# Splitting the weights one expert ahead and taking the first batch in two halves, in an attention and expert-MLP kernel

## What is computed

```
a  = layernorm(x);  xn = layernorm(a) * gamma + beta
q, k, v = split(xn @ w_qkv);  k = softmax over the tokens(k)      # 4 heads of 32
att = (k^T v per head) applied to q, @ w_out + b_out
x1 = x + layernorm(att + a)
h  = layernorm(x1)
x2 = x1 + layernorm(sum over 8 experts of (silu(h @ Wg[e]) * (h @ Wu[e])) @ Wd[e])
```

## Time and profile before

| | |
|---|---|
| median of 3 runs | 592.81 us (592.29 to 592.82) |
| the profiled execution | 592.07 us |
| its span in the trace | 590.3 us |
| TensorE busy (matmuls) | 583.4 us, 99% of the span |
| VectorE, ScalarE, GpSimd busy | 74%, 59%, 29% |

### The profile page before, as it was taken

The page is one execution under the profiler, slowest core; times in us unless marked ns, Lnnn a source line. Parts: engine busy times, 40 slices in busy tenths (PEclk is TensorE's granted clock), DMA queues, the critical chain, the costliest instruction groups (busy, mean ns, idle before and its releaser), DMA issues.

```text
span 590.3 us, 9190 instructions
## 1 busy us (share of the span) xinstructions
PE 583.4 (99%) x2627; PEld 462.7 (78%) x2627; DVE 437.8 (74%) x975; ACT 346.0 (59%) x619; POOL 170.8 (29%) x205
## 2 busy tenths in 40 slices
PE   9999999999999999999999999999999999999996
PEld 5677887788877888778878788778887788888885
DVE  5877885798667985779756887678875787668666
ACT  5778666545574555745557556654567545555554
POOL 4997680037001370015500353004610032001001
PEclk9999999999999999999999999999999999999999
DMA  5522110201101020100202002020110201010000
GB/s 164 159 75 89 37 36 1 73 19 54 37 36 37 19 70 22 59 31 1 89 0 72 18 19 71 1 72 19 37 37 0 73 18 37 1 37 18 2 0 19
DMA packets 28032, 24.46 MB, mean 41 GB/s; under 512 B 3024, under 2 KB 20944, under 8 KB 27984
## 3 DMA queue, kind: packets, MB, share of 16 engines
q1 hardware_dynamic: 27408, 23.73, 12.5%
q10 hardware_dynamic: 576, 0.20, 0.1%
HBM read 15.27 MB, written 8.65 MB: 41 GB/s over the span
## 4 chain that ended last, share of the span: by engine, by line
PE 96%; ACT 1%; DVE 1%; issue 1%; POOL 0%; POOLq 0%; DVEq 0%; ACTq 0%
PE gate_ps L985 10%; PE gate_ps L988 10%; PE up_ps L988 10%; PE acc_ps L988 10%; PE gate_ps L986 10%; PE up_ps L985 10%; PE acc_ps L985 10%; PE up_ps L986 10%; PE acc_ps L986 10%; PE att_ps L1066 1%; PE att_ps L1077 1%; PE att_ps L1052 1%; PE up_ps L1125 1%; PE att_ps L1043 0%; PE att_ps L1073 0%
## 5 line engine op out<-in xcount | busy, mean ns | idle before, releaser
L587 ACT ACTIVATE gs<-gate_ps 128x512 f32<-128x512 f32 x255 | 152.4, 598 | 217.0 <-PE gate_ps L988 215.8
L795 DVE TENSOR_TENSOR h<-gs,up_ps 128x512 f32<-128x512 f32 x255 | 174.8, 685 | 131.3 <-PE up_ps L988 119.2
L782 DVE TENSOR_TENSOR h_lo<-h,h_hi 128x512 fp32r<-128x512 f32 x255 | 187.8, 736 | 0.1
L564 ACT ACTIVATE h_hi<-h 128x512 fp32r<-128x512 f32 x255 | 159.4, 625 | 8.9 <-DVE h L795 8.9
L985 PE MATMUL gate_ps<-x1nT_hi,wg_hi 128*128 128x512 f32 (+1 forms) x256 | 106.6, 416 | 0.0
L988 PE MATMUL up_ps<-x1nT_lo,wu_hi 128*128 128x512 f32 (+1 forms) x256 | 101.4, 396 | 0.0
L988 PE MATMUL gate_ps<-x1nT_lo,wg_hi 128*128 128x512 f32 (+1 forms) x256 | 101.4, 396 | 0.0
L985 PE MATMUL up_ps<-x1nT_hi,wu_hi 128*128 128x512 f32 (+1 forms) x256 | 101.0, 395 | 0.0
L988 PE MATMUL acc_ps<-h_lo,wd_hi 128*128 128x512 f32 x254 | 100.8, 397 | 0.0
L986 PE MATMUL gate_ps<-x1nT_hi,wg_lo 128*128 128x512 f32 (+1 forms) x256 | 100.6, 393 | 0.0
L986 PE MATMUL up_ps<-x1nT_hi,wu_lo 128*128 128x512 f32 (+1 forms) x256 | 100.5, 393 | 0.0
(11 more groups left out here) (228 smaller groups left out, 492.3 us busy)
## 6 DMA issues: line engine op xcount, KB each, us to landing
w_raw<-in_L_ffn_Wg_dram SPq DMA_DIRECT2D x8, 256.0 KB, 2.8
w_raw<-in_L_ffn_Wu_dram SPq DMA_DIRECT2D x8, 256.0 KB, 2.8
w_raw<-in_L_ffn_Wd_dram SPq DMA_DIRECT2D x8, 256.0 KB, 3.2
x_in<-in_L_attn_x_dram SPq DMA_DIRECT2D x7, 256.0 KB, 2.6
t_dram_acc<-t_blk_acc SPq DMA_DIRECT2D x7, 256.0 KB, 2.3
t_out_acc<-t_dram_acc SPq DMA_DIRECT2D x28, 64.0 KB, 2.0
out_dram<-res SPq DMA_DIRECT2D x7, 256.0 KB, 2.1
t_dram_x<-t_blk_x SPq DMA_DIRECT2D x6, 256.0 KB, 2.1
```

Of the source, the lines that this page charges most:

```text
L564: act.activation(h_hi[s % NH][:, :], h[s % NGU][:, :], ACT.Copy).then_inc(s_hhi, 1)
L587: act.activation(gs[q][:, :], gate_ps[q][:, :], ACT.Silu).then_inc(s_silu, 1)
L782: dve.tensor_tensor(h_lo[s % NH][:, :], h[s % NGU][:, :], h_hi[s % NH][:, :].bitcast(F32), ALU.subtract).then_inc(s_hlo, 1)
L795: dve.tensor_tensor(h[q][:, :], gs[q][:, :], up_ps[q][:, :], ALU.mult).then_inc(s_h, 1)
```

## The change

It has these parts. `FIRST` becomes 1: only expert 0 is split in the prologue, and each later expert 4 steps later than before (expert e from step 4(e-1) on), on ScalarE and GpSimd; the tables of the attention stay. GpSimd's low part 1 moves ahead of the powers of z and x1. The steps 0 and 1 of the MLP (`EARLY = 2`) run in halves, the first half's high products ahead of the second half's transposes. In the prologue the first two tiles go ahead of the last two through the statistics, variance and mean of x, z and x1; x1 is made in SBUF and its copy falls away; one of each pair of x1n tiles is made by ScalarE in two instructions; the last y tile moves from ScalarE to VectorE; a residual matmul moves behind the matmuls of A; and 20 fillers on zeros become 10 matmuls on weight data in five forms and 3 on zeros. The load of batch 2's x waits for the x1 sums and no longer for their copies.

```diff
@@ -38,10 +38,12 @@
-BUSY = {"start": 8, "w": 5, "attn": 20}
-FIRST = 2
+BUSY = {"start": 8, "w": 5}
+FIRST = 1
+EARLY = 2
@@ -359,7 +362,7 @@
                 if m == 8:
-                    sp.wait_ge(s_f_x1, J)
+                    sp.wait_ge(s_f_x1ps, J)
                     load_x(2, 0)
@@ -495,17 +498,18 @@
                 toks = slice(i * JH, i * JH + JH)
-                pool.wait_ge(s_f_y, i * JH + JH)
+                pool.wait_ge(s_f_y, JH + i)
+                if i == 1:
+                    pool.wait_ge(s_f_y_dve, 1)
                 pool.tensor_tensor(yb[:, toks, :], y[:, toks, :], bout_bc[:, :].rearrange("p (a d) -> p a d", a=1)
...
             split_lo(pool, 0)
+            split_lo(pool, 1)
             half_power("z", 0)
             half_power("z", 1)
-            split_lo(pool, 1)
             half_power("x1", 0)
             half_power("x1", 1)
-            for m in range(2, 3 * FIRST):
-                split_lo(pool, m)
+            split_lo(pool, 2)
             bodies(pool, body)
@@ -630,10 +634,9 @@
             act.activation(Ek[:, JH:, :], gate_ps[0][:, HALF], ACT.Copy).then_inc(s_f_E2, 1)
-            residual(3)
+            split_hi(0)
             act.wait_ge(s_f_qT_ps, 1)
             act.activation(qT[:, :], acc_ps[:, :], ACT.Copy).then_inc(s_f_qT, 1)
-            split_hi(0)
             split_hi(1)
@@ -641,12 +644,24 @@
                                    bias=nm["z"][:, j:j + 1], scale=1.0).then_inc(s_f_zc, 1)
-            for m in range(3, 3 * FIRST):
-                split_hi(m)
             act.wait_ge(s_mask, 3)
...
+            def first_x1n(i):
+                j = i * JH + 1
+                act.wait_ge(s_f_nm, 3 + i)
+                act.activation(x1n[:, j, :], x1[0][:, j, :], ACT.Identity, bias=nm["x1"][:, j:j + 1],
+                               scale=1.0).then_inc(s_f_zc, 1)
+                act.wait_ge(s_f_zc, J + 1 + i)
+                act.wait_ge(s_f_rstd["x1"], i + 1)
+                act.activation(x1n[:, j, :], x1n[:, j, :], ACT.Copy,
+                               scale=rstd["x1"][:, 0, j:j + 1]).then_inc(s_f_x1n_act, 1)
+            first_x1n(0)
             act.wait_ge(s_f_n, 1)
             act.activation(x1nT_hi[0][:, HALF], att_ps[:, HALF], ACT.Copy).then_inc(s_f_hi, 1)
+            first_x1n(1)
             act.wait_ge(s_f_n, 2)
@@ -846,11 +861,11 @@
             first_stats("x", 1, x_in[0][:, 1, :])
+            first_aggregate("x", 0)
+            first_variance("x", 0, 1)
             dve.wait_ge(s_xb, 16)
             first_stats("x", 2, x_in[0][:, 2, :])
-            first_aggregate("x", 0)
             first_stats("x", 3, x_in[0][:, 3, :])
-            first_variance("x", 0, 1)
             first_aggregate("x", 1)
@@ -872,6 +887,9 @@
             dve.tensor_reduce(kmax_neg[:, 0:1], att_ps[:, :], AX_X, ALU.max, negate=True).then_inc(s_f_kmax, 1)
+            dve.wait_ge(s_f_nmr, 1)
+            dve.tensor_scalar(y[:, J - 1, :], x_in[0][:, J - 1, :], rstd["x"][:, 0, J - 1:J], nmr[:, J - 1:J], ALU.mult,
+                              ALU.add).then_inc(s_f_y_dve, 1)
             dve.wait_ge(s_f_T, 1)
@@ -889,64 +907,57 @@
-            def z_mean(i):
+            def half_mean(k, i):
                 toks = slice(i * JH, i * JH + JH)
-                dve.tensor_scalar(nm["z"][:, toks], mv["z"][:, toks, 0], -1.0, None, ALU.mult).then_inc(s_f_nm, 1)
-            for j in range(3):
-                dve.wait_ge(s_f_z, j + 1)
-                first_stats("z", j, tile_banks[j][:, 0:D])
-            first_aggregate("z", 0)
-            dve.wait_ge(s_f_z, 4)
-            first_stats("z", 3, tile_banks[3][:, 0:D])
-            first_variance("z", 0)
-            z_mean(0)
-            first_aggregate("z", 1)
-            first_variance("z", 1)
-            z_mean(1)
+                dve.tensor_scalar(nm[k][:, toks], mv[k][:, toks, 0], -1.0, None, ALU.mult).then_inc(s_f_nm, 1)
+            for i in range(2):
+                for j in range(i * JH, i * JH + JH):
+                    dve.wait_ge(s_f_z, j + 1)
+                    first_stats("z", j, tile_banks[j][:, 0:D])
+                first_aggregate("z", i)
+                first_variance("z", i)
+                half_mean("z", i)
...
                 dve.wait_ge(s_f_zc, j + 1)
-                dve.scalar_tensor_tensor(out=tile_banks[j][:, D:2 * D], in0=tile_banks[j][:, 0:D],
+                dve.scalar_tensor_tensor(out=x1[0][:, j, :], in0=tile_banks[j][:, 0:D],
                                          scalar=rstd["z"][:, 0, j:j + 1], in1=x_in[0][:, j, :], op0=ALU.mult,
...
                 dve.wait_ge(s_f_x1ps, j + 1)
-                first_stats("x1", j, tile_banks[j][:, D:2 * D])
+                first_stats("x1", j, x1[0][:, j, :])
...
                 dve.wait_ge(s_f_rstd["x1"], j // JH + 1)
-                dve.tensor_scalar(x1n[:, j, :], tile_banks[j][:, D:2 * D], mv["x1"][:, j, 0:1],
-                                  rstd["x1"][:, 0, j:j + 1], ALU.subtract, ALU.mult).then_inc(s_f_x1n, 1)
+                dve.tensor_scalar(x1n[:, j, :], x1[0][:, j, :], mv["x1"][:, j, 0:1], rstd["x1"][:, 0, j:j + 1],
+                                  ALU.subtract, ALU.mult).then_inc(s_f_x1n, 1)
...
             first_x1_stats(1)
+            first_aggregate("x1", 0)
+            first_variance("x1", 0)
+            half_mean("x1", 0)
             first_x1(2)
-            first_aggregate("x1", 0)
             first_x1(3)
-            first_variance("x1", 0)
             first_x1_stats(2)
+            first_x1n(0)
             first_x1_stats(3)
...
             first_variance("x1", 1)
-            first_x1n(0)
-            first_x1n(1)
-            first_x1n(2)
-            first_x1n(3)
+            half_mean("x1", 1)
             dve.wait_ge(s_f_hi, 1)
...
                               ALU.subtract).then_inc(s_f_lo, 1)
+            first_x1n(2)
             dve.wait_ge(s_x1nT_hi, 1)
...
                               ALU.subtract).then_inc(s_x1nT_lo, 1)
-            for j in range(J):
-                dve.wait_ge(s_f_x1ps, j + 1)
-                dve.tensor_copy(x1[0][:, j, :], tile_banks[j][:, D:2 * D]).then_inc(s_f_x1, 1)
@@ -996,27 +1007,9 @@
                     pe.wait_ge(s_wlo, 3 * e + 2)
-                if first and s == 0:
-                    kinds = [(w_hi[k][:, e, cols], w_lo[k][:, e, cols], ps[q], done)
-                             for k, ps, done in ((0, gate_ps, s_gate), (1, up_ps, s_up))]
-                    for half, hi_made, lo_made in ((HALF, s_f_hi, s_f_lo), (REST, s_x1nT_hi, s_x1nT_lo)):
-                        pe.wait_ge(hi_made, 1)
-                        for hi, lo, ps, _ in kinds:
-                            pe.matmul(ps[:, half], hi, x1nT_hi[par][:, half], start=True, stop=False)
-                            pe.matmul(ps[:, half], lo, x1nT_hi[par][:, half], start=False, stop=False)
-                        pe.wait_ge(lo_made, 1)
-                        for hi, _, ps, done in kinds:
-                            last = pe.matmul(ps[:, half], hi, x1nT_lo[par][:, half], start=False, stop=True)
-                            if half is REST:
-                                last.then_inc(done, 1)
-                    return
                 for k, ps, s_done, s_free in ((0, gate_ps[q], s_gate, s_silu), (1, up_ps[q], s_up, s_h)):
...
                         pe.wait_ge(s_free, t - since(s, NGU) + 1)
-                    elif s:
-                        pe.wait_ge(s_f_x1, 2 * s - 1 if k == 0 else 2)
                     products(ps[:, :], w_hi[k][:, e, cols], w_lo[k][:, e, cols], x1nT_hi[par][:, :],
@@ -1025,8 +1018,6 @@
                     pe.wait_ge(s_wlo, 3 * e + 3)
-                if first and s == 0:
-                    pe.wait_ge(s_f_x1, J)
                 pe.wait_ge(s_hhi, t + 1)
@@ -1109,7 +1100,8 @@
                     t = b * STEPS + s
-                    gate_up(t, b, s, par, first)
+                    if not first or s >= EARLY:
+                        gate_up(t, b, s, par, first)
                     if s >= LAG:
@@ -1180,17 +1172,17 @@
             pe.matmul(up_ps[0][:, 2 * D:3 * D], bm[:, :], wout[:, :], start=True, stop=True).then_inc(s_R_ps, 1)
-            pe.wait_ge(s_f_yb, 1)
-            residual(0)
             pe.wait_ge(s_f_E, 1)
...
             last.then_inc(s_f_A_ps, 1)
+            pe.wait_ge(s_f_yb, 1)
+            residual(0)
+            residual(1)
             pe.wait_ge(s_U, 1)
             pe.wait_ge(s_U2, 1)
-            residual(1)
             pe.wait_ge(s_f_A, 1)
@@ -1201,12 +1193,53 @@
                           stop=True).then_inc(s_f_z, 1)
-            keep_busy(BUSY["attn"])
-            for j in range(J):
-                pe.wait_ge(s_f_x1n, j + 1)
-                last = pe.transpose((att_ps, up_ps[2])[j // JH][:, j % JH * P:j % JH * P + P], x1n[:, j, :], ident[:, :])
-                if j % JH == JH - 1:
-                    last.then_inc(s_f_n, 1)
+            w0, w1 = w_hi[0][:, 0, :], w_hi[0][:, 0, 0:P]
+            pe.wait_ge(s_whi, 1)
```

(42 more changed lines are left out.)

## The result

The changed kernel takes 605.05 us (median of 6 runs, 604.18 to 605.57), the kernel before 592.55 in the same comparison (6 runs, 592.07 to 592.91): a ratio of 1.0208, 95% interval 1.0197 to 1.0219. It is slower, as forecast, by 12.5 us instead of 8.7, and 605.05 lies 0.15 above the upper end of the range. The profiled execution took 605.3 us with a span of 603.5, 13.2 longer than the span before.

The account below looks back on a forecast made before the run. TensorE was taken to bound the kernel, busy 583.4 of 590.3 us. Waits of 2.0 (after the prologue's 1.0 gain) + 3.55 + 3.2 = 8.75, say 8.7 longer, gave 601.5 us; range 598.8 to 604.9.

Parts of the forecast that it names:

- The splits: MLP: with FIRST 1, GpSimd's low parts come late and TensorE waits; 2.0 + 3.55 + 3.2 = 8.75 us longer.
- All four waits: TensorE waiting for GpSimd's low parts at steps 8, 23, 24 and 28: 2.3, 1.3, 2.3 and 3.2 us.
- Step 4: MLP step 4 wants low part 4: TensorE waits 0.2 to 0.7 us, taken 0.5.
- The prologue: Ahead of the MLP: step 2 starts at 22.4, 1.0 us sooner (0 to 1.6); first silu at 22.1, not sooner.
- (a): x transposes: first half's statistics ahead of the wait for the second half give back 0.25 us (0 to 0.25).
- (c): z: one statistic and an aggregate fewer ahead of the first variance; GpSimd's power begins at 14.5 instead of 15.15.
- (d): x1: first x1n begins at 17.8 instead of 18.63, ScalarE's tile ends at 18.3, TensorE starts at 19.2.
- (e): Steps 0 and 1: eight high products (0.12 each) cover the second half's x1n; second half's start at 21.0, step 2 at 22.4.
- rival 3: TensorE returns from waits at half clock: 1.8 us each, twice 3.6, 605.1; before the MLP up to 1, 602.5; chance 14%.
- its own case: The forecast's main case for the whole kernel: 599.0 to 604.3 us, chance 73%.
- Rivals 1 and 2: MLP waits: GpSimd gets ahead, only the prologue's gain remains, 591.8, 4%; or the two late waits are met, 594.8 to 598.4, 9%.
- Rival 4: Prologue gains nothing, halves bound by the same powers: first silu and all behind up to 0.5 later, 602.0; no separate chance.

Follow-up runs that it names:

- experiment 8: Kernel before with only FIRST = 1, plus matmuls on zeros (8, 8, 10) ahead of TensorE's waits at steps 8, 24 and 28: 601.66 us, ratio 1.0156.
- experiment 4: Changed kernel with matmuls on zeros (10, 8, 8) ahead of TensorE's waits at steps 8, 24 and 28: 603.94 us, ratio 1.0196.
- experiment 1: Changed kernel with FIRST back at 2, all else as changed: 594.18 us, ratio 1.0025.
- experiment 2: Kernel before with FIRST = 1 and nothing else: 604.69 us, ratio 1.0192.
- experiment 3: Changed kernel, fillers edited: (a) ten on weight data replaced by eleven on zeros, 605.74 us; (b) three more on zeros, 605.5 us.
- experiment 5: Changed kernel with FIRST = 2, silu table loaded earlier, three more fillers, second transposes earlier, low part 2 later, high part 3 moved: 592.18 us, ratio 0.9995.
- experiment 7: Changed kernel, from expert 2 on high parts two steps sooner and low parts in the same step as the high ones: 596.8 us, ratio 1.0077.

## Why the prediction was partly right

By differences of medians the 12.5 us are 9.3 for the late splits at full clock (experiment 8), 1.1 for the clock behind the waits (605.05 - 603.94), and 2.1 that are left for the new prologue (experiment 4's 603.94 less before, 11.4, less that 9.3). The first of the three is measured by itself. The other two depend on the order in which they are taken, and the sum closes only because the last is what is left. Alone, the new prologue costs 1.7 (experiment 1). With before's prologue the clock costs 2.9 (12.2 in experiment 2 less 9.3 in experiment 8), and the new prologue on top of that adds only 0.3. In experiment 2's trace a slow stretch lay behind step 28, where no later wait takes it up: step 29 came 4.10 behind step 28, where it was 2.45 before.

- **The splits: right.** All four waits came where they were forecast, and 8.7 became 9.3: the mechanism held, and the size is 0.6 short. GpSimd's power of the next batch comes 6.49 behind the first silu, as forecast (30.92 - 24.43); from there to the end of low part 5 it is 36.51 - 30.92 = 5.59, for 5.58. The two subtractions then took 3.35 instead of 3.0: both were long. At step 23 the wait is 1.31, for 1.3. To step 24 it was again one long and one short. From step 24 to 28 it is 11.25, for 11.6: x1n took 1.85 where the earlier trace rows had 2.71. The wait at step 28 itself was 1.06 and not 3.2, since the slow stretch behind step 24 had used up a part of it. ve_x at step 24 took 0.17, as forecast for an idle GpSimd.
- **Step 4: right**, 0.46 for 0.5, and ended by low part 4.
- **The prologue: wrong.** The forecast had the first silu at 22.1 and step 2 at 22.4; they came at 24.43 and 24.59. From the first silu to step 8 it is 15.5 us for 15.2, so 2.3 of the 2.7 us by which step 8 came later than forecast hang on the silu. The terms: (a) gave the 0.25 at the x transposes, and z still began 0.35 later than before (13.80), as the first five fillers took 1.59 instead of 1.14 us in the chain; the start-up rise of the clock came later. TensorE's list is the same in both kernels up to there, so this is a difference between executions and not of the change: in the eleven traces of this case the same five fillers took from 1.24 to 2.12 us in the timeline. (c) z to the power took 1.49 for 1.4. (d) had the table load too early: ScalarE's load of the silu table ran from 16.82 to 18.10, and x1n's two passes behind it ended at 19.04 where I had 18.3. So the first product came at 19.99 and not 19.2. (e) was the largest miss, at 1.3 us: the eight high products of 256 columns took 1.84 us, most of them 0.21 each, not 0.96 at 0.12, and the second transposes stood behind them, so that the second half's high products came at 23.11 and not 21.0. The lines for (d) and (e):

```profile
16.82 1.28 ACT L648 ACT_TABLE_LOAD   x1
...
19.99 0.55 PE L1224 MATMUL gate_ps<-x1nT_hi,wg_hi 128*128 128x256 f32 x1 [0.57 <-ACT x1nT_hi L663]
...
21.83 0.63 PE L1215 MATMUL up_ps<-ident,x1n 128*128 128x128 f32 x2
...
23.11 0.32 PE L1224 MATMUL gate_ps<-x1nT_hi,wg_hi 128*128 128x256 f32 x1
```

  The forecast had named this loss, as a fallen clock in front of the MLP, inside rival 3, and gave its own case none of it. The clock is not all of it: with the clock up (experiment 3) step 2 still came at 23.82 and 23.40, 1.0 and more behind the forecast's 22.4.
- **A mended prologue is worth 0.2 at step 2, not 1.0** (experiment 5), and nothing that can be told from zero at the end. The 1.0 was read from a sum of best cases over four engines.
- **Rival 3, the clock: right in mechanism.** Its price of 1.8 a time fits the stretch behind step 8 (1.6). Its "twice" does not: behind step 24 the slow matmuls used up a wait that was there anyway. Its 605.1 is near the result by luck: the prologue's loss stands in for the second time. With before's prologue the clock did cost nearly twice its 1.6, 2.9 us (experiments 2 and 8). By the Trainium skill (TensorE: Matmul & The Clock Gate, section "HAM oscillation — how this bites in real kernels"), idle gaps between bursts of matmuls bring TensorE back at half rate; the windows of the changed kernel and of experiment 4 agree, 0.57 behind an idle wait and 1.00 behind a filled one.
- **Rivals 1 and 2** fall: none of the four waits was met. **Rival 4** had the sign of the prologue right and its size wrong (0.5, for 1.7 alone or 2.1 in the sum above).
- **The range** left out the case in which the clock falls and the prologue fails together. Whether the two go together isn't shown. The prologue's loss comes in part from the table load and from the order of TensorE's list, and what lowers the clock there stays open.
- **Marks that misled.** The wait list named "issue" for three waits for which the forecast promised w_lo, and ScalarE's wd_hi for the one at step 4; the ends of the low parts settled all four. TensorE's busy time rose by 5.2 instead of falling by 1.6: twelve products of 256 columns were some 0.09 longer each and fifteen of 512 columns 0.20, together 4.1 us of the 6.8 between the two.

Open: what brings the clock down in front of the MLP, the fillers' forms, the gap behind them, or neither (experiment 3); how the loss is shared between the prologue and the clock, beyond the bounds above; and why a slow stretch is eight matmuls in one execution and thirteen in another.

## What to carry to other kernels

Where work moves to a later place in an engine's list, read from the old trace when the item that had that place ended, and compare it with when the consumer wants the moved one, item by item; here this gave 8.7 us where 9.3 were measured. A wait of about 2 us on TensorE, where it bounds the kernel, cost its length here and most times the clock behind it too, unless a later wait took up the loss; cheap matmuls in the wait bought the clock back and narrowed the spread. When shares are read from differences of runs, the order in which they are taken can change them: the clock's was 1.1 or 2.9 us here. A gain that needs four engines to hand over at their best should be priced by the slowest hand-over, with the table loads that stand in the list written out.

## What the runs showed of the hardware

- A VectorE scaling of 128x128 fp32 from SBUF to SBUF took 1.15 us beside a GpSimd subtraction and 0.34 with it held back; read from PSUM it took 0.41 beside the same subtraction. Putting x1 in SBUF made this. The Trainium skill (SBUF — State Buffer, section "Who interferes with whom") says that such an instruction can take a mode that uses both of VectorE's port pairs, one of which GpSimd shares, and that whichever comes first holds it for its whole instruction. The trace agrees as far as it is exact: the scaling ended at 21.37, 0.08 behind the subtraction (20.01 + 1.28). A scaling of 128x4 was held likewise, 1.02 instead of 0.17 us, and ended 0.03 behind the subtraction beside it (experiment 7).
- Behind waits of 2.0 to 2.6 us TensorE was granted 0.50 of its clock (1.2 GHz) for six to thirteen matmuls of 512 columns, though not behind each of them (step 24 of experiment 2 kept it), and the first slow one was the first to the sixth behind the wait. Behind the changed kernel's waits of 1.31 and 1.06 us, and in the MLP behind fillers and a rest of 0.2 to 0.9 (experiments 4 and 8), it stayed at 1.00. In front of the MLP it fell behind fillers and gaps of 0.74 and 0.57 us, and in experiment 3 (a) it stayed up behind gaps of 0.79 and 0.56.
- The start-up rise to 2.4 GHz came some 0.4 us later in the changed kernel's profiled execution than in the one before, and moved all that follows. It differs between executions: the five fillers in which it falls took 1.24 us in five traces and 2.12 in one.
